# A four-layer image pipeline on one core: six of eight scan convolutions move from TensorE to GpSimd

## The chip, the cores and the metric

One core of a Trainium2 chip runs the program. Its engines work side by side, each through its own queue in order: TensorE (PE, with weight loads shown as PEld), VectorE (DVE), ScalarE (ACT), GpSimd (POOL) and SyncE (SP), which here issues the DMAs. The metric is the device time of one execution in microseconds (us), the median of several.

## The reference

The input is 16 images of 64 channels and 16 x 16 pixels. Four layers follow: an attention over channels; a deformable 3x3 convolution (offsets from a convolution, bilinear samples, batch norm, relu); a softmax attention over the 256 pixels; and a block with layer norm, a depthwise 3x3 convolution, four gated one-dimensional scans, a fuse matmul, a second layer norm and a gated feed-forward. The scans are what this change is about. For each of four directions (left to right, right to left, top to bottom, bottom to top):

```python
y = depthwise 5-tap convolution of seq along the row (or the column) + dw_b
g = sigmoid(seq @ g_w.T + g_b)
o = o + y * g            # then fuse_w, and added to x
```

seq is the depthwise convolution's result, here called y.

## The kernel before

Two images make a pair: their 2 x 64 channels fill the 128 partitions, 256 pixels lie along the row, and there are eight pairs. Each pair runs through some fifty steps. What each engine does, and in which order, is written out by hand in PLAN: a list of tokens step.pair for each engine, walked once. Every step waits on semaphores for its inputs and raises one when it is done. Steps of several pairs are interleaved: while one pair is sampled, the pair before is in its attention and the one before that in its scans. An engine can't pass a waiting step: what stands behind it in the list waits too.

The steps that matter here, with n the pair:

- sp0 to sp8 spread interpolation weights by matmul, ScalarE copies half of them (xe0 to xe8), VectorE multiplies (w0a to w8b, L901, one operand from PSUM, the other from SBUF), and PE samples with the products (s0a to s8b, L534). w8b.n is a pair's last product and s8b.n its last sample. Then relu.n (ScalarE, L747), qk2.n, logit.n, max.n (VectorE, L907, L910), the exponentials, nrm0.n and nrm1.n (the softmax's division, L920), et.n, av.n, x3.n.
- ln1.n: statistics on VectorE, five short 128x1 instructions on GpSimd (L1046 to L1055), the normalization on ScalarE into z_pad. dw.n: two taps of the depthwise convolution on ScalarE; dw2.n to dw8.n: seven on VectorE (L942), each a scalar_tensor_tensor with two SBUF operands. y.n: the two sums added (L951) into y_pad, an image with a border of two.
- gate.n: four matmuls (L602), tanh on ScalarE. scan.n (L615): for each of two axes, five taps, two images, one matmul of 256 columns with a diagonal matrix as weights, two directions side by side in the 128 output partitions; a float32 matmul is two instructions, so 40 in all. ScalarE evicts the scan with its bias into conv (L808). prod.n (VectorE, L957): (tanh + 1) x conv, both in SBUF. fuse.n, x4.n, ln2.n, ff.n, u.n, ff2.n, out.n and the store end the pair.
- dist.n, abs.n, hat.n, hat_y.n (L877, L885) and low.n make the interpolation weights of a later pair. low.n (L1039) is five instructions on GpSimd, whose result feeds PE's transposes tr0.n to tr2.n. x1.n on GpSimd is a copy (L1033).
- hot and warm are matmuls on zeros that fill PE's gaps at both ends.

SP loads x in pairs and stores y_out, each in its order. z_pad, y_pad, dw_acc, gates, conv, prod, z2 and the feed-forward's tiles exist once, so a pair's step waits for the pair before to have used them.

## Time and profile before

| | before |
|---|---|
| median of 3 runs (lowest to highest) | 303.65 us (303.65 to 304.49) |
| span of the profiled execution | 301.8 us |
| PE busy | 287.8 us, 95% |
| VectorE busy | 213.0 us, 71% |
| ScalarE busy | 190.4 us, 63% |
| GpSimd busy | 53.0 us, 18% |
| TensorE clock granted | full in every slice |

The profile is one execution; its own time is the span, and what lies between it and the runs' median is outside the program's instructions. Busy time is the union of an engine's instructions. A timeline row gives the start, the duration, the engine, the line of the kernel, the operation, what it writes and reads, and a count where equal ones are merged; in brackets how long the engine was idle before and who ended it. The chain of waits goes back from the last instruction to what released it, at each step.

### The profile page before, as it was taken

The page shows a single profiled execution, that of the slowest core. Times are in us where ns is not written, and L with a number is a line of the kernel's source. Part 1 is how long each engine was busy: PE and PEld are TensorE (multiplying, and loading weights), DVE is VectorE, ACT ScalarE, POOL GpSimd, SP SyncE. Part 2 cuts the span into 40 slices and gives each one's busy share as a digit, 9 for nine tenths or more (in the row PEclk, how much of TensorE's full clock was granted, in tenths as well). Part 3 has the DMA queues.
Part 4 walks back from the last instruction along what each step waited for, and adds up shares of the span by engine and source line. Part 5 has one row for each costly group of instructions (what it writes and reads, how often), then busy time and mean ns, then how long its engine had stood idle before and what let it go on. Part 6 is the DMA issues. An engine that isn't in the chain of part 4 may idle for free.

```text
span 301.8 us, 7399 instructions
## 1 busy us (share of the span) xinstructions
PE 287.8 (95%) x2870; PEld 183.7 (61%) x2870; DVE 213.0 (71%) x424; ACT 190.4 (63%) x399; POOL 53.0 (18%) x139
## 2 busy tenths in 40 slices
PE   7798999999999999999999999999999999989995
PEld 3555567567555765575767566675565656657742
DVE  3173984779799788858877827687998996655342
ACT  1268757867886569837685654866975755564332
POOL 0332040400140215010222100301421011011110
PEclk9999999999999999999999999999999999999999
DMA  7300000000000000100010001000000000000001
GB/s 235 140 0 20 0 22 2 2 0 2 0 2 3 3 1 2 35 2 0 3 35 2 3 0 31 8 2 1 2 2 0 21 0 3 17 2 0 2 17 35
DMA packets 3057, 4.98 MB, mean 16 GB/s; under 512 B 336, under 2 KB 2768, under 8 KB 2896
## 3 DMA queue, kind: packets, MB, share of 16 engines
q1 hardware_dynamic: 3024, 4.52, 4.7%
q8 instruction: 23, 0.38, 0.6%
q14 instruction: 10, 0.08, 0.1%
HBM read 3.47 MB, written 1.05 MB: 15 GB/s over the span
## 4 chain that ended last, share of the span: by engine, by line
PE 85%; DVE 5%; ACT 5%; issue 3%; POOL 1%; ACTq 0%; POOLq 0%; DVEq 0%
PE ps_cv L534 22%; PE ps_pair L615 11%; PE ps_yb L494 8%; PE ps_pair L480 7%; PE ps_ma L437 6%; PE ps_ma L464 4%; PE ps_mb L580 3%; PE ps_pair L602 3%; PE ps_pair L570 3%; PE ps_mb L591 3%; PE ps_mb L547 3%; PE ps_mb L388 2%; PE ps_pair L635 2%; PE ps_mb L624 2%; PE ps_yb L374 1%
## 5 line engine op out<-in xcount | busy, mean ns | idle before, releaser
L901 DVE TENSOR_TENSOR sb_wt<-ps_yb,sb_xe 128x512 f32<-128x512 f32 x144 | 94.0, 684 | 26.4 <-PE ps_xb L489 24.9
L534 PE MATMUL ps_cv<-sb_wt,sb_w_x 128*64 128x256 f32 x576 | 77.3, 385 | 0.0
L740 ACT ACTIVATE sb_xe<-ps_xb 128x512 f32<-128x512 f32 x72 | 43.0, 597 | 19.3 <-PE ps_xb L489 19.2
L534 PEld LDWEIGHTS ps_cv<-sb_wt,sb_w_x 128*64 128x64 f32 x576 | 38.2, 136 | 20.2 <-issue 7.5
L615 PE MATMUL ps_pair<-sb_y_pad,sb_par 64*128 64x256 f32 x320 | 37.4, 383 | 0.3 <-ACT sb_gates L799 0.3
L615 PEld LDWEIGHTS ps_pair<-sb_y_pad,sb_par 64*128 64x128 f32 x320 | 30.9, 184 | 5.8 <-issue 2.5
L942 DVE SCALAR_TENSOR_TENSOR sb_dw_acc<-sb_z_pad,sb_par,sb_dw_acc 128x256 f32<-128x256 f32 x56 | 25.2, 480 | 9.4 <-ACT sb_dw_acc L792 5.3
L494 PE MATMUL ps_yb<-sb_hats,sb_sel 32*128 32x512 f16 x144 | 29.8, 383 | 0.7
L1039 POOL TENSOR_TENSOR sb_parts<-sb_hat,sb_parts 128x256 f16<-128x256 f32 (+2 forms) x40 | 23.3, 615 | 38.7 <-ACT sb_parts L710 38.6
L1046 POOL TENSOR_SCALAR sb_sc<-sb_mv 128x1 f32<-128x1 f32 x16 | 3.0, 190 | 142.1 <-DVE sb_mv L936 74.7
L489 PE MATMUL ps_xb<-sb_hats,sb_sel 32*128 32x512 f16 x72 | 27.7, 385 | 0.2 <-ACT sb_hats L719 0.2
L730 ACT ACTIVATE sb_w_x<-ps_pair 128x1024 f32<-128x1024 f32 (+1 forms) x24 | 19.4, 810 | 7.7 <-PE ps_pair L480 7.5
L480 PE MATMUL ps_pair<-sb_par,sb_x 64*128 64x256 f32 (+1 forms) x192 | 23.4, 361 | 0.6 <-ACT sb_w_x L730 0.3
L719 ACT ACTIVATE sb_hats<-ps_ma 128x1024 f16<-128x1024 f16 (+1 forms) x24 | 21.1, 880 | 1.7 <-PE ps_ma L464 1.5
L494 PEld LDWEIGHTS ps_yb<-sb_hats,sb_sel 32*128 32x128 f16 x144 | 7.3, 91 | 21.2 <-issue 17.0
L480 PEld LDWEIGHTS ps_pair<-sb_par,sb_x 64*128 64x128 f32 x192 | 15.5, 185 | 7.3 <-issue 6.7
L808 ACT ACTIVATE sb_conv<-ps_pair,sb_par 128x512 f32<-128x512 f32 x16 | 10.1, 683 | 13.1 <-PE ps_pair L615 13.0
L437 PE MATMUL ps_ma<-sb_x_pad,sb_par 128*64 128x128 f32 x288 | 17.4, 274 | 0.3 <-ACT sb_hats L719 0.3
L437 PEld LDWEIGHTS ps_ma<-sb_x_pad,sb_par 128*64 128x64 f32 x288 | 15.8, 136 | 2.3 <-issue 1.6
L769 ACT ACTIVATE sb_b_exp<-ps_pair,sb_b_neg 128x256 f32<-128x256 f32 x32 | 14.8, 473 | 3.0 <-DVE sb_b_neg L910 2.7
L872 DVE TENSOR_TENSOR sb_dist<-ps_ma,sb_grid 128x1152 f32<-128x1152 f32 x8 | 10.8, 1354 | 6.2 <-PE ps_ma L446 6.2
L464 PE MATMUL ps_ma<-sb_sel,sb_parts 128*64 128x128 f16 x320 | 13.8, 222 | 0.0
(117 smaller groups left out, 438.4 us busy)
## 6 DMA issues: line engine op xcount, KB each, us to landing
sb_par<-in_par SPq DMA_DIRECT2D x1, 1519.5 KB, 7.7
sb_x_in<-in_x SPq DMA_DIRECT2D x8, 128.0 KB, 2.1
out_y<-sb_y_out SPq DMA_DIRECT2D x8, 128.0 KB, 1.7
sb_par<-in_par SPq DMA_DIRECT2D x1, 397.0 KB, 4.0
sb_par<-in_par SPq DMA_DIRECT2D x1, 192.0 KB, 3.4
sb_par<-in_par SPq DMA_DIRECT2D x1, 128.0 KB, 2.2
sb_sel<-in_sel SPq DMA_DIRECT2D x1, 128.0 KB, 3.9
```

The lines of the kernel that those rows point to most:

```text
L437: mm = nc.tensor.matmul(ma[C * h:C * (h + 1), 0:P], par_sb[:, a + 2 * OM * t:a + 2 * OM * (t + 1)], x1_pad[:, r:r + HALF_ROWS, t % 3:t % 3 ...
L464: mm = nc.tensor.transpose(bk[columns_of(t), at:at + P], parts[:, 2 * h + b, 4 * g + 2 * t:4 * g + 2 * (t + 1), :, :], ident16)
L480: mm = nc.tensor.matmul(pair[:, 512 * b + PIX * h:512 * b + PIX * h + k], x1[r, P * h:P * (h + 1)], par_sb[r, a:a + k], start=True, stop=True)
L489: return nc.tensor.matmul(xb[:, :], sel_sb[rows, P:2 * P], hats[n % 2][rows, g, :], start=True, stop=True)
L494: return nc.tensor.matmul(yb[h][:, :], sel_sb[rows, P * (2 + h):P * (3 + h)], hats[n % 2][rows, g, :], start=True, stop=True)
L534: mm = nc.tensor.matmul(cv[C * b:C * (b + 1), 0:PIX], w_x[n % 2][:, b, h, k, :], wt_of(n, k, h)[:, PIX * b:PIX * (b + 1)], start=(k == 0 a ...
L615: mm = nc.tensor.matmul(pair[:, 512 * b + PIX * d:512 * b + PIX * (d + 1)], par_sb[r, a:a + P], rows, start=(j == 0), stop=(j == KS - 1))
L719: nc.scalar.activation(hats[n % 2][:, g0:g1, :].rearrange("p g q -> p (g q)"), ma[:, :].bitcast(F16)[:, 0:k], ACT.Copy).then_inc(ev(f"hats ...
L740: nc.scalar.activation(xe[t % XE][:, :], xb[:, :], ACT.Copy).then_inc(ev("xe_ok"), 1)
L901: nc.vector.tensor_tensor(wt_of(n, k, h)[:, :], yb[h][:, :], xe[t % XE][:, :], ALU.mult)\
L942: nc.vector.scalar_tensor_tensor(out=sum_of, in0=dw_source(t), scalar=col("dw_w", t), in1=sum_of, op0=ALU.mult, op1=ALU.add).then_inc(ev(f ...
L1039: nc.gpsimd.tensor_tensor(parts[:, 0:g, a:b, 1, :], hat[:, 0:g, a:b, :], parts[:, 0:g, a:b, 0, :], ALU.subtract).then_inc(ev("low_ok"), 1)
```

## The change

For pairs 1 to 6 the scan is done by GpSimd instead of by PE and ScalarE; pairs 7 and 8 stay as they were. y.n then goes into a plain tile y. GpSimd needs both directions of an axis in the two halves of the partitions, so SP issues four DMAs (dup.n), which copy each image's 64 channels of y to both halves of y_dup. For each axis GpSimd multiplies the middle tap with its weight and adds the bias (mul0), then multiplies each of the four other taps into a scratch tile (mul1 to mul4) and adds it to the sum (sum1 to sum4): 18 instructions a pair over two axes, of 512, 480 or 448 columns, since a tap that reaches past the border is cut. mul13.2 is axis 1, fourth tap, pair 2. prod.n waits for the last sum on both axes. y_pad, z_pad, dw_acc, gates, conv, prod, z2 and the feed-forward's tiles are doubled, x4 has three buffers, x2 eight; the waits look two or three pairs back accordingly, and some waits on older steps are written out. All four orders are new, SP has one of its own, and the zero matmuls at the end are fewer (25 pairs instead of 46). The core of the diff:

```diff
-    ("scan_w", 2 * KS * P), ("scan_b", 2), ("gate_w", 2 * P), ("gate_b", 2), ("fuse_w", C),
+    ("scan_w", 2 * KS * P), ("scan_b", 2), ("scan_c", 2 * KS), ("gate_w", 2 * P), ("gate_b", 2), ("fuse_w", C),
...
+        s1a.8 s1b.8 ff2.4 sp4.8 s2a.8 s2b.8 fuse.5 s3a.8 s3b.8 s4a.8 sp5.8 et1.7 tr2.8 s4b.8 et0.7 sp6.8 ff.5 s5a.8
+        sp7.8 s5b.8 av.7 s6a.8 sp8.8 gate.6 s6b.8 s7a.8 sp_last.8 s7b.8 ff2.5 s8a.8 s8b.8 hot.1 qk2.8 hot.2 logit.8 v2.8
+        hot.3 fuse.6 hot.4 et0.8 gate.7 et1.8 hot.5 av.8 scan.7 hot.6 ff.6 hot.7 gate.8 fuse.7 hot.8 scan.8 ff2.6 hot.9
+        ff.7 fuse.8 hot.10 ff2.7 hot.11 ff.8 hot.12 ff2.8
...
+        w6a.5 out.2 w6b.5 w7a.5 x3.4 st1.4 w7b.5 w8a.5 qk.7 w8b.5 dw2.4 dw4.4 w0a.6 a_max.7 prod.3 a_norm.7 dw6.4 w0b.6
+        x4.3 w1a.6 dw3.4 st2.3 dw5.4 dw8.4 dw7.4 y.4 w1b.6 w2a.6 w2b.6 w3a.6 x1.7 w3b.6 u.3 w4a.6 dist.7 w4b.6 out.3
+        hat.7 hat_y.7 qk.8 w5a.6 w5b.6 w6a.6 a_max.8 a_norm.8 w6b.6 w7a.6 max.5 w7b.6 w8a.6 x1.8 nrm0.5 prod.4 w8b.6
+        w0a.7 nrm1.5 w0b.7 w1a.7 dist.8 w1b.7 w2a.7 x3.5 st1.5 hat.8 w2b.7 w3a.7 hat_y.8 dw2.5 w3b.7 dw3.5 w4a.7 dw5.5
+        dw4.5 w4b.7 dw6.5 dw7.5 max.6 w5a.7 dw8.5 x4.4 y.5 st2.4 w5b.7 w6a.7 nrm1.6 w6b.7 nrm0.6 w7a.7 w7b.7 w8a.7 x3.6
+        st1.6 w8b.7 w0a.8 u.4 w0b.8 w1a.8 dw2.6 dw3.6 dw4.6 w1b.8 dw5.6 dw6.6 w2a.8 dw8.6 dw7.6 w2b.8 y.6 w3a.8 max.7
+        prod.5 out.4 w3b.8 w4a.8 x4.5 nrm1.7 st2.5 w4b.8 nrm0.7 w5a.8 w5b.8 w6a.8 w6b.8 w7a.8 x3.7 st1.7 w7b.8 w8a.8 u.5
+        w8b.8 dw2.7 out.5 dw4.7 dw6.7 dw3.7 dw5.7 prod.6 max.8 dw7.7 dw8.7 x4.6 nrm0.8 y.7 nrm1.8 st2.6 x3.8 st1.8 dw2.8
...
+        grid.1 x1.1 low.1 x1.2 low.2 bn.1 x1.3 x1.4 low.3 ln1.1 low.4 mul10.1 mul00.1 mul11.1 mul01.1 sum01.1 sum11.1
+        x1.5 mul12.1 mul02.1 sum12.1 mul13.1 sum13.1 ln1.2 sum02.1 mul03.1 mul14.1 sum03.1 sum14.1 mul04.1 sum04.1 low.5
+        ln2.1 mul00.2 mul10.2 mul01.2 sum01.2 mul02.2 mul11.2 sum02.2 ln1.3 sum11.2 mul12.2 mul03.2 sum12.2 sum03.2
+        mul13.2 sum13.2 mul04.2 mul14.2 sum04.2 sum14.2 mul10.3 mul00.3 mul11.3 mul01.3 x1.6 sum01.3 sum11.3 mul02.3
+        mul12.3 ln2.2 sum02.3 mul03.3 sum03.3 mul04.3 sum12.3 low.6 sum04.3 ln1.4 mul13.3 sum13.3 mul14.3 sum14.3 ln2.3
+        mul00.4 mul10.4 mul11.4 x1.7 sum11.4 mul01.4 mul12.4 sum12.4 sum01.4 mul02.4 mul13.4 sum02.4 sum13.4 low.7
+        mul14.4 mul03.4 sum03.4 mul04.4 sum04.4 sum14.4 x1.8 ln1.5 low.8 ln2.4 mul10.5 mul11.5 sum11.5 mul00.5 mul01.5
+        mul12.5 sum12.5 ln1.6 sum01.5 mul13.5 mul02.5 sum02.5 mul03.5 sum13.5 sum03.5 mul04.5 mul14.5 sum04.5 sum14.5
+        mul10.6 mul11.6 mul00.6 mul01.6 sum11.6 sum01.6 ln2.5 mul12.6 mul02.6 sum02.6 sum12.6 mul13.6 mul03.6 sum03.6
+        ln1.7 mul04.6 sum13.6 mul14.6 sum04.6 sum14.6 ln2.6 ln1.8 ln2.7 ln2.8
+    """,
+    "sp": """
+        load.3 load.4 load.5 dup.1 load.6 dup.2 dup.3 load.7 load.8 store.1 dup.4 dup.5 dup.6 store.2 store.3 store.4
+        store.5 store.6 store.7 store.8
     """,
...
-HOT = {1: 4, 2: 2, 3: 3, 4: 2, 5: 5, 6: 5, 7: 8, 8: 13, 9: 4}
+BY_POOL = (1, 2, 3, 4, 5, 6)
+ORDER = (2, 1, 3, 0, 4)
+SUMS = 2 * KS - 1
+BY_PE = tuple(n for n in range(1, PAIRS + 1) if n not in BY_POOL)
+HOT = {1: 1, 2: 2, 3: 1, 4: 3, 5: 1, 6: 3, 7: 3, 8: 1, 9: 1, 10: 4, 11: 1, 12: 4}
...
+def done_count(name, n):
+    return sum(k <= n for k in BY_PE) if name == "scan" else n
...
-        z_pad = sb("z_pad", [P, H + 2, PW])
-        dw_acc = [sb(f"dw_acc{i}", [P, PIX]) for i in range(2)]
-        y_pad = sb("y_pad", [P, H + 4, SW])
-        gates = sb("gates", [P, 2, 2, PIX])
-        conv = sb("conv", [P, 2, 2, PIX])
-        prod = sb("prod", [P, 2, 2, PIX])
-
-        x4 = [sb(f"x4{i}", [P, PIX]) for i in range(2)]
+        z_pad = [sb(f"z_pad{i}", [P, H + 2, PW]) for i in range(2)]
+        dw_acc = [[sb(f"dw_acc{i}{t}", [P, PIX]) for t in range(2)] for i in range(2)]
+        y_pad = [sb(f"y_pad{i}", [P, H + 4, SW]) for i in range(2)]
+        y = [sb(f"y{i}", [P, PIX]) for i in range(2)]
+        y_dup = [sb(f"y_dup{i}", [P, 2, H, W]) for i in range(2)]
+        tap_of = [sb(f"tap_of{i}", [P, 2 * PIX]) for i in range(2)]
+        gates = [sb(f"gates{i}", [P, 2, 2, PIX]) for i in range(2)]
+        conv = [sb(f"conv{i}", [P, 2, 2, PIX]) for i in range(2)]
+        prod = [sb(f"prod{i}", [P, 2, 2, PIX]) for i in range(2)]
+
+        x4 = [sb(f"x4{i}", [P, PIX]) for i in range(3)]
         st2, mv2, sc2 = sb("st2", [P, 6]), sb("mv2", [P, 2]), sb("sc2", [P, 5])
-        z2 = sb("z2", [P, PIX])
-        ff_a = sb("ff_a", [P, 2, PIX])
-        ff_g = sb("ff_g", [P, 2, PIX])
-        ff_u = sb("ff_u", [P, 2, PIX])
+        z2 = [sb(f"z2{i}", [P, PIX]) for i in range(2)]
+        ff_a = [sb(f"ff_a{i}", [P, 2, PIX]) for i in range(2)]
+        ff_g = [sb(f"ff_g{i}", [P, 2, PIX]) for i in range(2)]
+        ff_u = [sb(f"ff_u{i}", [P, 2, PIX]) for i in range(2)]
...
+        def made_by(pairs, n):
+            return sum(m <= n for m in pairs)
+
+        def scan_step(n, d, j):
+            return SUMS * made_by(BY_POOL, n) - SUMS + j + 1
...
-            for n in range(3, PAIRS + 1):
-                if n > 5:
-                    store(n - 5)
-                load(n)
-            for n in range(PAIRS - 4, PAIRS + 1):
-                store(n)
+            def dup(n):
+                sp.wait_ge(ev("y_ok"), n)
+                for d in range(2):
+                    wait_past(sp, ev(f"scan_step{d}"), SUMS * made_by(BY_POOL, n - 2))
+                for b in range(2):
+                    for i in range(2):
+                        sp.dma_start(y_dup[n % 2][C * i:C * (i + 1), b, :, :].rearrange("p h w -> p (h w)"),
+                                     y[n % 2][C * b:C * (b + 1), :])\
+                            .then_inc(dup_ok[n % 2], 16)
+
+            walk(PLAN["sp"], {"load": load, "store": store, "dup": dup})
...
-                                              y_pad[r, 2:2 + H, 2:2 + W], start=True, stop=True)
+                                              image(y[n % 2][:, :])[r, :, :] if n in BY_POOL else y_pad[n % 2][r, 2:2 + H, 2:2 + W],
+                                              start=True, stop=True)
...
             def gate(n):
                 act.wait_ge(ev("gate_mm"), n)
-                wait_past(act, ev("prod_ok"), n - 1)
+                wait_past(act, ev("prod_ok"), n - 2)
                 for d in range(2):
-                    last = nc.scalar.activation(gates[:, d, :, :],
+                    last = nc.scalar.activation(gates[n % 2][:, d, :, :],
                                                 pair[:, :].rearrange("p (b d q) -> p b d q", b=2, d=2)[:, :, d, :],
                                                 ACT.Tanh, bias=gate_bh[:, d:d + 1], scale=0.5)
                 last.then_inc(ev("gate_ok"), 1)
 
             def scan(n):
-                act.wait_ge(ev("scan_mm"), n)
-                wait_past(act, ev("prod_ok"), n - 1)
+                act.wait_ge(ev("scan_mm"), made_by(BY_PE, n))
+                wait_past(act, ev("prod_ok"), n - 2)
                 for d in range(2):
-                    last = nc.scalar.activation(conv[:, d, :, :],
+                    last = nc.scalar.activation(conv[n % 2][:, d, :, :],
                                                 pair[:, :].rearrange("p (b d q) -> p b d q", b=2, d=2)[:, :, d, :],
                                                 ACT.Identity, bias=col("scan_b", d))
                 last.then_inc(ev("scan_ok"), 1)
...
             def dw_sum(n):
-                wait_past(dve, ev("gate_mm"), n - 1)
-                wait_past(dve, ev("scan_mm"), n - 1)
+                wait_past(dve, ev("gate_mm"), n - 2)
+                wait_past(dve, ev("scan_mm"), made_by(BY_PE, n - 2))
+                if n - 2 in BY_POOL:
+                    dve.wait_ge(dup_ok[n % 2], 64 * len([m for m in BY_POOL if m <= n - 2 and (n - m) % 2 == 0]))
                 dve.wait_ge(ev("dw_step1"), dw_count(n, TAPS - 2))
                 dve.wait_ge(ev("dw_step0"), dw_count(n, TAPS - 1))
-                nc.vector.tensor_tensor(y_pad[:, 2:2 + H, 2:2 + W], image(dw_acc[0][:, :]), image(dw_acc[1][:, :]),
-                                        ALU.add).then_inc(ev("y_ok"), 1)
+                to = image(y[n % 2][:, :]) if n in BY_POOL else y_pad[n % 2][:, 2:2 + H, 2:2 + W]
+                nc.vector.tensor_tensor(to, image(dw_acc[n % 2][0][:, :]), image(dw_acc[n % 2][1][:, :]), ALU.add).then_inc(ev("y_ok"), 1)
 
             def prod_step(n):
+                wait_past(dve, ev("fuse_mm"), n - 2)
                 dve.wait_ge(ev("gate_ok"), n)
-                dve.wait_ge(ev("scan_ok"), n)
-                nc.vector.scalar_tensor_tensor(out=prod[:, :, :, :].rearrange("p d b q -> p (d b q)"),
-                                               in0=gates[:, :, :, :].rearrange("p d b q -> p (d b q)"), scalar=1.0,
-                                               in1=conv[:, :, :, :].rearrange("p d b q -> p (d b q)"),
+                if n in BY_POOL:
+                    for d in range(2):
+                        dve.wait_ge(ev(f"scan_step{d}"), scan_step(n, d, SUMS - 1))
+                else:
+                    dve.wait_ge(ev("scan_ok"), made_by(BY_PE, n))
+                nc.vector.scalar_tensor_tensor(out=prod[n % 2][:, :, :, :].rearrange("p d b q -> p (d b q)"),
+                                               in0=gates[n % 2][:, :, :, :].rearrange("p d b q -> p (d b q)"), scalar=1.0,
+                                               in1=conv[n % 2][:, :, :, :].rearrange("p d b q -> p (d b q)"),
                                                op0=ALU.add, op1=ALU.mult).then_inc(ev("prod_ok"), 1)
...
-            nc.vector.memset(z_pad[:, :, :], 0.0).then_inc(zero_ok, 1)
-            nc.vector.memset(y_pad[:, :, :], 0.0).then_inc(zero_ok, 1)
+            for i in range(2):
+                nc.vector.memset(z_pad[i][:, :, :], 0.0).then_inc(zero_ok, 1)
+                nc.vector.memset(y_pad[i][:, :, :], 0.0).then_inc(zero_ok, 1)
...
+            def scan_rows(n, d, j):
+                at, to = max(0, j - KS // 2), max(0, KS // 2 - j)
+                m = H - at - to
+                if d == 0:
+                    return (y_dup[n % 2][:, :, :, at:at + m].rearrange("p b h w -> p (b h) w"),
+                            conv[n % 2][:, d, :, :].rearrange("p b (h w) -> p (b h) w", h=H)[:, :, to:to + m],
+                            tap_of[d][:, 0:2 * H * m].rearrange("p (k w) -> p k w", w=m))
+                return (y_dup[n % 2][:, :, at:at + m, :].rearrange("p b h w -> p b (h w)"),
+                        conv[n % 2][:, d, :, W * to:W * (to + m)],
+                        tap_of[d][:, 0:2 * W * m].rearrange("p (b k) -> p b k", b=2))
+
+            def scan_times(d, i):
+                def step(n):
+                    rows, sum_of, tap_to = scan_rows(n, d, ORDER[i])
+                    weight = col("scan_c", KS * d + ORDER[i])
+                    if i == 0:
+                        pool.wait_ge(dup_ok[n % 2], 64 * len([k for k in BY_POOL if k <= n and (n - k) % 2 == 0]))
+                        wait_past(pool, ev("prod_ok"), n - 2)
+                        nc.gpsimd.tensor_scalar(sum_of, rows, weight, col("scan_b", d), ALU.mult, ALU.add)\
+                            .then_inc(ev(f"scan_step{d}"), 1)
+                    else:
+                        pool.wait_ge(ev(f"scan_step{d}"), scan_step(n, d, 2 * i - 2))
+                        nc.gpsimd.tensor_scalar(tap_to, rows, weight, None, ALU.mult).then_inc(ev(f"scan_step{d}"), 1)
+                return step
+
+            def scan_plus(d, i):
+                def step(n):
+                    rows, sum_of, tap_to = scan_rows(n, d, ORDER[i])
+                    pool.wait_ge(ev(f"scan_step{d}"), scan_step(n, d, 2 * i - 1))
+                    nc.gpsimd.tensor_tensor(sum_of, sum_of, tap_to, ALU.add).then_inc(ev(f"scan_step{d}"), 1)
...
+    d["scan_c"] = taps.reshape(2, 2, KS, C).transpose(1, 3, 0, 2).reshape(P, 2 * KS)
```

## Rows read from the trace of the kernel before

**Rows 1.** The page, first table: busy time, share, instructions.
```profile
span 301.8 us, 7399 instructions
PE 287.8 (95%) x2870; PEld 183.7 (61%) x2870; DVE 213.0 (71%) x424; ACT 190.4 (63%) x399; POOL 53.0 (18%) x139
```

**Rows 2.** Timeline of VectorE: w8b.3 and w8b.8 (start, us, engine, line).
```profile
96.83 0.69 DVE L901 TENSOR_TENSOR sb_wt<-ps_yb,sb_xe 128x512 f32<-128x512 f32 x1
...
252.33 0.69 DVE L901 TENSOR_TENSOR sb_wt<-ps_yb,sb_xe 128x512 f32<-128x512 f32 x1 [0.49 <-PE ps_yb L494]
```

**Rows 3.** Busy time of each engine from w8b.3 to w8b.8.
```profile
core 0: us, PE busy (x) PEld busy (x) DVE busy (x) ACT busy (x) POOL busy (x), PEclk, DMA share, GB/s
97.53:253.02 155.49, 154.45 (x1533) 99.11 (x1531) 123.74 (x244) 106.74 (x223) 28.08 (x74) 1.00 0.03 7
```

**Rows 4.** Chain of waits behind the last sample (start, us, what).
```profile
253.84 1.29 PE ps_cv L534 x12
...
255.56 4.61 PE ps_pair L615 x40
260.18 1.01 PE ps_mb L547 x8
...
282.70 4.70 PE ps_pair L615 x40
```

**Rows 5.** Groups by line and shape: xcount | busy us, mean ns | idle before.
```profile
L808 ACT ACTIVATE sb_conv<-ps_pair,sb_par 128x512 f32<-128x512 f32 x16 | 10.1, 683 | 13.1 <-PE ps_pair L615 13.0
...
L957 DVE SCALAR_TENSOR_TENSOR sb_prod<-sb_gates,sb_conv 128x1024 f32<-128x1024 f32 x8 | 9.7, 1218 | 0.3 <-ACT sb_conv L808 0.3
...
L747 ACT ACTIVATE sb_x<-ps_cv,sb_bn_s 128x256 f32<-128x256 f32 x8 | 4.5, 557 | 2.6 <-PE ps_cv L534 2.6
```

**Rows 6.** Groups by line and shape, GpSimd.
```profile
L1039 POOL TENSOR_TENSOR sb_parts<-sb_hat,sb_parts 128x256 f16<-128x256 f32 x28 | 18.2, 680 | 34.1 <-ACT sb_parts L710 34.0
...
L1051 POOL TENSOR_TENSOR sb_sc<-sb_sc,sb_par 128x1 f32<-128x1 f32 x16 | 3.6, 223 | 1.3
L1033 POOL COPY sb_x<-sb_x_pad 128x256 f32<-128x256 f32 x8 | 3.4, 421 | 54.8 <-DVE sb_x_pad L863 40.1 <-PE ps_pair L480 14.7
L1046 POOL TENSOR_SCALAR sb_sc<-sb_mv 128x1 f32<-128x1 f32 x16 | 3.0, 190 | 142.1 <-DVE sb_mv L936 74.7 <-DVE sb_mv L972 67.5
...
L1024 POOL TENSOR_TENSOR sb_grid<-sb_par 128x1152 f32<-128x1152 f32 x1 | 2.1, 2150 | 0.0
```

**Rows 7.** DMA issues (KB each, us to landing).
```profile
sb_x_in<-in_x SPq DMA_DIRECT2D x8, 128.0 KB, 2.1
out_y<-sb_y_out SPq DMA_DIRECT2D x8, 128.0 KB, 1.7
```

**Rows 8.** Timeline of SP: what one issue takes.
```profile
1.15 0.43 SPq L326 DMA_DIRECT2D sb_x_in<-in_x  x1
```

**Rows 9.** Timeline of VectorE and GpSimd at three places.
```profile
112.84 0.76 DVE L877 TENSOR_SCALAR sb_hat<-sb_hat 128x1152 f32<-128x1152 f32 x1 [0.29 <-ACT sb_hat L704]
112.93 0.72 POOL L1051 TENSOR_TENSOR sb_sc<-sb_sc,sb_par 128x1 f32<-128x1 f32 x1
114.31 1.28 DVE L901 TENSOR_TENSOR sb_wt<-ps_yb,sb_xe 128x512 f32<-128x512 f32 x2
...
192.10 2.95 POOL L1039 TENSOR_TENSOR sb_parts<-sb_hat,sb_parts 128x256 f16<-128x256 f32 x5 [9.94 <-ACT sb_parts L710]
193.94 0.76 DVE L856 TENSOR_SCALAR sb_a_nrm<-sb_a_exp,sb_a_rec 128x64 f32<-128x64 f32 x1
...
217.27 3.20 POOL L1039 TENSOR_TENSOR sb_parts<-sb_hat,sb_parts 128x256 f16<-128x256 f32 x5 [0.29 <-ACT sb_parts L710]
217.62 0.34 DVE L910 TENSOR_SCALAR sb_b_neg<-sb_b_max 128x4 f32<-128x4 f32 x1
219.07 0.47 DVE L942 SCALAR_TENSOR_TENSOR sb_dw_acc<-sb_z_pad,sb_par,sb_dw_acc 128x256 f32<-128x256 f32 x1
```

**Rows 10.** Two lines of VectorE: duration ns min/median/max.
```profile
L856 DVE TENSOR_SCALAR sb_a_nrm<-sb_a_exp,sb_a_rec x8: 253/254/762, 8.6 to 193.9; 128x64 f32<-128x64 f32 x8
...
L910 DVE TENSOR_SCALAR sb_b_neg<-sb_b_max x8: 169/169/339, 68.4 to 264.7; 128x4 f32<-128x4 f32 x8
```

194 lines of the change are left out of this document (100 added, 94 removed).

## The prediction

> **What bounds the kernel now.** I read the page's first table: PE is busy for 95% of the span, no other engine above 71% [rows 1]. A mean can hide stages, so I cut the span where the order of the work cuts it, at the end of the last weight product of a pair (w8b) on VectorE: w8b.3 ends at 97.53 us, w8b.8 at 253.02 [rows 2]. In that stretch of 155.49 us (B) PE is busy for 154.45 and VectorE for 123.74, the granted clock is 1.00, that is 2.4 GHz, and GpSimd has 28.08 [rows 3]. So PE alone sets B; five of the eight scans (pairs 1 to 5) lie in it. Ahead of it (A, 97.53 us) there is no scan. Behind it (C, 48.8 us) the chain of waits shows pair 8's latency: its last sample, then 4.61 us of scan.6, which has nothing to do with pair 8 but stands ahead of qk2.8 in PE's order, then qk2, logits, softmax, layer norm, depthwise convolution, scan.8, the rest [rows 4].
>
> The profiled execution's own time is the 301.8 us span; the median of the runs is 303.65, so 1.85 us lies around it, which I leave as it is.
>
> **The change part by part.**
>
> *PE loses six scans.* One takes 4.61 us from its first matmul to the next step's, whether in B or C [rows 4]. In B PE keeps 154.45 - 5 x 4.61 = 131.4, with its 1.04 us of idle time 132.4. ScalarE loses twelve evictions of 0.68 us [rows 5], 8.2 us of an engine that has 106.74 in B [rows 3]; no gain by itself.
>
> *GpSimd gains 18 instructions per pair*: ten multiplications of 448 to 512 columns (mean 474) and eight additions (mean 464). No row has these. For the addition I take the two-input forms: 0.68 us at 256 columns, 2.15 at 1152, 1.64 ns per column, so 1.02 us. For the multiplication the copy: 0.42 at 256, against 0.19 for a multiplication of one column, 0.9 ns per column, so 0.6 [rows 6]. Together 10 x 0.6 + 8 x 1.02 = 14.2 us. Bounds: all 18 at the copy's price, 10.8; all at the addition's, 18.4. I keep 14.2, since each form is priced by its nearest row. The Trainium skill (GPSIMD Engine Reference, Engine selection) calls one-input operations roughly line-rate on GpSimd; at its 1.2 GHz that is an estimate of 0.4 us for the multiplication, under what the copy's rows give, and the scan would be near 12 us.
>
> *The copies of y.* Four DMA issues of 0.43 us each and some 2.1 us to landing, as the loads of x [rows 7, 8]: 3.4 us from y to the first multiplication. SP has long waits, so its time is free; store.2 to store.8 move behind dup.6, but y_out is double, and out.4, the first that needs store.2, stands behind y.6, max.7, prod.5 (1.22 us by itself [rows 5]) and a weight product, against issues and a landing of 1.7 [rows 7, 8]. I cost that at nothing; without that cover it is under 2 us once.
>
> *VectorE's own work.* In the new order B holds 1.8 us more of it (one x4 with its statistics, one u): 125.5. That is under PE's 132.4. But the rows show that the two engines exclude each other. A 128x1 step of GpSimd that takes 0.19 [rows 6] took 0.72 beside VectorE's hat instruction, and ended 0.05 us behind it; five splits took 3.20 instead of 2.95 with one depthwise step among them [rows 9]. The other way round, VectorE's a_nrm (0.25) took 0.76 and b_neg (0.17) took 0.34 while GpSimd split hats [rows 9, 10]. The weight products, which read one operand from PSUM, ran beside GpSimd at their usual length (1.28 for two) [rows 9]. So what counts is VectorE's instructions with two SBUF operands, and its fast tensor_scalar. By the new order there are 86 in B: 35 depthwise steps, 5 y, 5 prod, 5 u, 8 hat, 20 of the softmax's division, 5 b_neg, 3 a_nrm. GpSimd would be at work for (5.5 x 14.2 + 28.08) / 150 = 0.70 of B. One that meets GpSimd waits for half of an instruction (time-weighted 0.87 us) less what its own start hides (b_neg had 0.31 us of GpSimd left and lost 0.17, so 0.14): 0.3 us. Sum 86 x 0.70 x 0.3 = 18 us; I take 17, 0.2 us each. Bounds: 0 (each begins in a gap), and 86 x 0.78 = 67 (each waits for a whole one).
>
> The Trainium skill (SBUF — State Buffer, Who interferes with whom) says that an instruction of VectorE with two SBUF inputs and one of GpSimd that reads SBUF hold a shared port exclusively, and that the second one blocks until the first is done. The rows agree (0.72 us instead of 0.19). Taken to the letter, with nothing hidden, it gives 86 x 0.70 x 0.43 = 26 us; that is the slower rival below.
>
> *A new wait.* prod.n waited for ScalarE's eviction; now it waits for GpSimd's last addition, and everything on VectorE stands behind it, weight products for PE too. Between y.4 and prod.4 VectorE has 14 weight products at 0.60 (two in 1.28, so 0.60 apart [rows 2, 9]) and 7.8 us else: 16.2, with eight lock waits 17.8. GpSimd needs 3.4 + 14.2, and in its order x1.7 and low.7 (0.4 + 3.1) lie in between: 21.1, with its gaps 22.5. So VectorE would wait some 4.7 us. The same count gives 1.7 for pair 1, nothing for 2, 1.3 for 3, 1.0 for 5, 2.6 for 6. One wait gives GpSimd a lead for the next, so of the 8.7 in B I take 6. As a whole GpSimd keeps up: six scans and the older steps between them are 113 us, with 127 gaps of 0.08 (1.3 us over 16 [rows 6]) 123, in some 155.
>
> *Deeper buffers and order* (z_pad, dw_acc, gates, conv, prod, z2, ff tiles, x4): they take out waits for the pair before. Idle PE is 1.04 us in B, so there is no more than that to win. The waits added on the older steps (attn_mm, logit_mm and such, of one or two pairs before) are over long before; nothing. Two more memsets, short ones, lie ahead of VectorE's first input, which comes only with qk.1; nothing.
>
> **The sum.** B: VectorE 125.5 + 17 + 6 + 1.0 idle, as PE has now, = 149.5 instead of 155.5: -6.0. C: qk2.8 no longer stands behind scan.6 but behind ScalarE's relu (0.56 us [rows 5] and its semaphores) and a short filler, so it starts 4.2 us earlier; but prod.6 now stands ahead of max.8 on VectorE and waits 2.6: -1.6. A: 0. 301.8 - 7.6 = 294.2, with 1.85 around it 296.0 us. At 149.5 against PE's 132.4, VectorE is what ends last.
>
> **The rivals.**
>
> 1. *PE stays the bound.* The locks cost little, because GpSimd's access is short or the order keeps the two apart. For it: in the trace of before only two of VectorE's instructions lost time. Against: GpSimd was at 18% then. B is 132.4, C -4.2: 303.65 - 23.1 - 4.2 = 276.4; with some locks, up to 289.
>
> 2. *Slower: the lock puts VectorE past the old time.* Place: the 86 instructions of B; price: 0.3 us each, as with nothing hidden, 26 us, and with it GpSimd's scans are later too, so all 8.7 us of waits at prod: 125.5 + 26 + 8.7 + 1 = 161.2, +5.7, C -1.6 at best: 308. It decides from 0.29 us per instruction on (125.5 + 25 + 6 + 1 = 157.5, two above B, less 1.6 in C). For it: a_nrm lost 0.51 us at once, since GpSimd went straight on from one split to the next; and 35 of the 86 stand directly behind another one. Against: depthwise steps that follow each other hold GpSimd back as well.
>
> 3. *GpSimd can't keep up.* Its queue is strict: low.6 and low.7, which feed PE's transposes, stand among scans 2 to 4. With 18.4 us per scan the whole is 138 + 10, still inside 155, but the waits at prod grow by 4.2 a pair, 20 us less what overlaps; half of it brings B to 159, the time to about 306. It has to be that dear, against the copy's row.
>
> **How the numbers follow.** A measurement of this kernel can tell about 0.3% (0.9 us) from no change. Forecast (289 to 302): 0.42. Rival 1 (276 to 289): 0.20. Rival 2 (302 to 316): 0.30. Rival 3: 0.08. The two slower ones reach back over no change: of their 0.38, 0.05 lies within 0.3%, and 0.33 above; 0.02 of the forecast's own lies within as well. Faster 0.60, same 0.07, slower 0.33. The range leaves out about 0.1 at either end: 281 to 310. The forecast's own is 289 to 302.
>
> **What would show it.** Right: PE's busy time 27 to 28 us lower with idle time in front of samples that wait for weight products; VectorE's depthwise steps at 0.6 to 0.9 us on average instead of 0.47 and its busy time 15 to 20 us higher; prod waiting for GpSimd; GpSimd at about 140 us; qk2.8 about 1 us after the last sample. Wrong: VectorE's steps unchanged and PE still above 95% (rival 1), or depthwise steps at 1 us and VectorE without gaps in a B above 155 us (rival 2); low.6 late and PE waiting for transposes (rival 3). If the granted clock falls below 1.00 with PE's gaps, the rows above don't hold.

## The result: 344.3 us, 13% slower

The changed kernel takes 344.29 us (343.12 to 345.19), the kernel before 304.07 us in the same runs: 1.132 times, 95% interval 1.129 to 1.136. The forecast was 296.

The page's first table of the changed kernel, then three lines of its 40 slices (PE's and GpSimd's busy tenths, and the granted clock in tenths), then the chain of work that ended last, in shares of the span:

```profile
span 343.4 us, 7077 instructions
PE 276.7 (81%) x2588; PEld 166.7 (49%) x2588; DVE 229.9 (67%) x426; ACT 184.8 (54%) x387; POOL 191.9 (56%) x247
...
PE   6879999999996569674878796799984959389874
...
POOL 2020220303179985999998179932479999923011
PEclk9899999999999659998799899699998789879999
...
POOL 38%; PE 37%; issue 10%; DVE 6%; ACT 5%; DMA 2%; SPq 2%; ACTq 0%; POOLq 0%; DVEq 0%
```

Against [rows 1] PE has fallen from 95% to 81%, GpSimd has risen from 53 to 192 us. Over the whole span no engine is near its limit, but GpSimd is at 9 tenths in most slices of the middle and leads the chain. I cut the span as in the prediction, at the last weight product of pairs 3 and 8. Stretch B of the changed kernel, the row that answers to [rows 3] (length; busy us and instructions of PE, weight loads, VectorE, ScalarE, GpSimd; granted clock; DMA):

```profile
98.45:293.09 194.64, 150.62 (x1320) 87.64 (x1320) 138.12 (x248) 102.64 (x213) 156.75 (x174) 0.89 0.05 12
```

B grew from 155.49 to 194.64 us, ahead of it 97.5 became 98.5 and behind it 48.8 became 50.3: the loss is in B. In it VectorE is busy for 138 and idle for 56. GpSimd's 156.75 us of work alone is more than the 149.5 us that I forecast for B. GpSimd's groups (line, operation, shape, count | busy, mean ns | idle before):

```profile
L1141 POOL TENSOR_SCALAR sb_tap_of<-sb_y_dup,sb_par 128x480 f32<-128x480 f32 x24 | 37.3, 1559 | 0.8
L1141 POOL TENSOR_SCALAR sb_tap_of<-sb_y_dup,sb_par 128x448 f32<-128x448 f32 x24 | 34.8, 1454 | 1.0
L1148 POOL TENSOR_TENSOR sb_conv<-sb_conv,sb_tap_of 128x480 f32<-128x480 f32 x24 | 28.7, 1205 | 0.6
L1148 POOL TENSOR_TENSOR sb_conv<-sb_conv,sb_tap_of 128x448 f32<-128x448 f32 x24 | 26.9, 1133 | 0.8
...
L1137 POOL TENSOR_SCALAR sb_conv<-sb_y_dup,sb_par 128x512 f32<-128x512 f32 x12 | 10.7, 895 | 18.2 <-DMA sb_y_dup<-sb_y 18.2
```

The multiplication of one input and one weight (L1141, 1.51 us on average) is dearer than the addition of two inputs (L1148, 1.17), and dearer than the multiplication that also adds the bias (L1137, 0.90 for more columns). A scan is 2 x 0.895 + 8 x 1.507 + 8 x 1.169 = 23.2 us.

What the engines waited for over the whole span (waiter <- releaser: us in total, times, longest):

```profile
ACT sb_z_pad L828 <- POOL sb_sc L1115: 26.8, 7, 6.5
DVE sb_dw_acc L992 <- ACT sb_dw_acc L833: 22.6, 7, 5.5
...
DVE sb_prod L1014 <- POOL sb_conv L1148: 10.9, 4, 3.6
...
PE ps_ma L499 <- POOL sb_parts L1099: 5.7, 3, 4.2
```

and the same waits at z_pad and at the first depthwise step before the change:

```profile
ACT sb_z_pad L785 <- POOL sb_sc L1055: 10.8, 6, 3.1
...
DVE sb_dw_acc L942 <- ACT sb_dw_acc L792: 5.3, 2, 2.7
...
DVE sb_dw_acc L942 <- ACT sb_dw_acc L790: 3.5, 2, 3.0
```

The largest is not prod. It is the layer norm: ln1's five short steps stand in GpSimd's list behind multiplications and additions of another pair's scan, ScalarE waits for them ahead of z_pad, and VectorE waits for ScalarE at the first depthwise step. One case, pair 2. VectorE's timeline ends the statistics at 102.79 us:

```profile
102.61 0.18 DVE L986 BATCH_NORM_AGGREGATE sb_mv<-sb_st 128x2 f32<-128x6 f32 x1
...
113.91 0.76 DVE L992 SCALAR_TENSOR_TENSOR sb_dw_acc<-sb_z_pad,sb_par,sb_dw_acc 128x256 f32<-128x256 f32 x1 [5.52 <-ACT sb_dw_acc L833]
...
121.47 1.61 DVE L1014 SCALAR_TENSOR_TENSOR sb_prod<-sb_gates,sb_conv 128x1024 f32<-128x1024 f32 x1 [3.01 <-POOL sb_conv L1148]
```

GpSimd's timeline meanwhile is at pair 1's scan, without a gap, and comes to ln1.2 at 110.96:

```profile
103.38 3.23 POOL L1141 TENSOR_SCALAR sb_tap_of<-sb_y_dup,sb_par 128x480 f32<-128x480 f32 x2
106.58 1.20 POOL L1148 TENSOR_TENSOR sb_conv<-sb_conv,sb_tap_of 128x480 f32<-128x480 f32 x1
107.87 1.79 POOL L1141 TENSOR_SCALAR sb_tap_of<-sb_y_dup,sb_par 128x448 f32<-128x448 f32 x1
109.75 1.12 POOL L1148 TENSOR_TENSOR sb_conv<-sb_conv,sb_tap_of 128x448 f32<-128x448 f32 x1
110.96 0.19 POOL L1106 TENSOR_SCALAR sb_sc<-sb_mv 128x1 f32<-128x1 f32 x1
```

So 1.3 us of work comes 8.2 us late, and VectorE is idle for 5.5 us there and for 3.0 more at prod.1. The same just behind B: pair 8's relu (L785) stands on ScalarE behind ln1.7's z_pad, which waits for GpSimd. VectorE waits for the same z_pad at the first depthwise step of pair 7, and out.5 (L1043) stands behind that step; out.5 reads a tile in PSUM that qk2.8 is to write:

```profile
296.55 0.60 ACT L828 ACTIVATE sb_z_pad<-sb_x,sb_sc 128x256 f32<-128x256 f32 x1 [4.21 <-POOL sb_sc L1115]
...
298.09 0.55 ACT L785 ACTIVATE sb_x<-ps_cv,sb_bn_s 128x256 f32<-128x256 f32 x1
...
297.82 1.45 DVE L992 SCALAR_TENSOR_TENSOR sb_dw_acc<-sb_z_pad,sb_par,sb_dw_acc 128x256 f32<-128x256 f32 x1 [4.73 <-ACT sb_dw_acc L833]
299.20 0.47 DVE L1043 SCALAR_TENSOR_TENSOR sb_y_out<-ps_mb,sb_par,sb_x 128x256 f32<-128x256 f32 x1
```

PE is idle for 5.4 us ahead of qk2.8, which begins 5.6 us after the last sample, where I had about 1. What ends the wait is out.5, a microsecond behind the relu:

```profile
299.82 1.97 PE L582 MATMUL ps_mb<-sb_x,sb_par 128*64 128x256 f32 x8 [5.36 <-DVE sb_y_out L1043]
```

### The profile page after: what moved, and what is told of

Same layout as the page of the kernel before. It is cut to its first block, busy times and chain, and to the rows that moved or that the text cites. A ratio compares the mean times of both kernels' runs of the same rounds, so it can differ in the third digit from the quotient of the medians.

```text
span 343.4 us, 7077 instructions
## 1 busy us (share of the span) xinstructions
PE 276.7 (81%) x2588; PEld 166.7 (49%) x2588; DVE 229.9 (67%) x426; ACT 184.8 (54%) x387; POOL 191.9 (56%) x247
## 4 chain that ended last, share of the span: by engine, by line
POOL 38%; PE 37%; issue 10%; DVE 6%; ACT 5%; DMA 2%; SPq 2%; ACTq 0%; POOLq 0%; DVEq 0%
POOL sb_tap_of L1141 17%; POOL sb_conv L1148 12%; PE ps_cv L569 8%; PE ps_pair L515 3%; PE ps_ma L472 3%; POOL sb_conv L1137 3%; PE ps_yb L529 3%; PE ps_pair L651 3%; PE ps_ma L499 2%; PE ps_pair L605 2%; DMA sb_y_dup<-sb_y 2%; SPq L377 2%; POOL sb_sc L1109 2%; PE ps_mb L582 1%; PE ps_yb L409 1%
## 5 line engine op out<-in xcount | busy, mean ns | idle before, releaser
L569 PE MATMUL ps_cv<-sb_wt,sb_w_x 128*64 128x256 f32 x576 | 85.3, 403 | 4.8 <-issue 3.3
L1141 POOL TENSOR_SCALAR sb_tap_of<-sb_y_dup,sb_par 128x480 f32<-128x480 f32 (+1 forms) x48 | 72.0, 1507 | 1.8
L1148 POOL TENSOR_TENSOR sb_conv<-sb_conv,sb_tap_of 128x480 f32<-128x480 f32 (+1 forms) x48 | 55.6, 1169 | 1.3
L992 DVE SCALAR_TENSOR_TENSOR sb_dw_acc<-sb_z_pad,sb_par,sb_dw_acc 128x256 f32<-128x256 f32 x56 | 32.5, 617 | 22.8 <-ACT sb_dw_acc L833 22.6
L515 PE MATMUL ps_pair<-sb_par,sb_x 64*128 64x256 f32 (+1 forms) x192 | 25.8, 390 | 10.8 <-ACT sb_w_x L769 7.4
L515 PEld LDWEIGHTS ps_pair<-sb_par,sb_x 64*128 64x128 f32 x192 | 16.9, 202 | 19.1 <-issue 14.3
L1137 POOL TENSOR_SCALAR sb_conv<-sb_y_dup,sb_par 128x512 f32<-128x512 f32 x12 | 10.7, 895 | 18.2 <-DMA sb_y_dup<-sb_y 18.2
L660 PE MATMUL ps_mb<-sb_prod,sb_fuse_h 128*64 128x256 f32 x64 | 10.4, 453 | 11.9 <-DVE sb_prod L1014 7.5
L472 PE MATMUL ps_ma<-sb_x_pad,sb_par 128*64 128x128 f32 x288 | 18.8, 285 | 0.7 <-DVE sb_x_pad L910 0.7
L828 ACT ACTIVATE sb_z_pad<-sb_x,sb_sc 128x256 f32<-128x256 f32 x8 | 4.8, 604 | 26.8 <-POOL sb_sc L1115 26.8
```

Source lines behind the costliest of these rows:

```text
L472: mm = nc.tensor.matmul(ma[C * h:C * (h + 1), 0:P], par_sb[:, a + 2 * OM * t:a + 2 * OM * (t + 1)], x1_pad[:, r:r + HALF_ROWS, t % 3:t % 3 ...
L515: mm = nc.tensor.matmul(pair[:, 512 * b + PIX * h:512 * b + PIX * h + k], x1[r, P * h:P * (h + 1)], par_sb[r, a:a + k], start=True, stop=True)
L569: mm = nc.tensor.matmul(cv[C * b:C * (b + 1), 0:PIX], w_x[n % 2][:, b, h, k, :], wt_of(n, k, h)[:, PIX * b:PIX * (b + 1)], start=(k == 0 a ...
L992: nc.vector.scalar_tensor_tensor(out=sum_of, in0=dw_source(n, t), scalar=col("dw_w", t), in1=sum_of, op0=ALU.mult, op1=ALU.add).then_inc(e ...
L1141: nc.gpsimd.tensor_scalar(tap_to, rows, weight, None, ALU.mult).then_inc(ev(f"scan_step{d}"), 1)
L1148: nc.gpsimd.tensor_tensor(sum_of, sum_of, tap_to, ALU.add).then_inc(ev(f"scan_step{d}"), 1)
```

## The experiments

All are built on the changed kernel (e4 on the one before). A lone `...` in a diff, or at the end of a line, marks code left out. "B" is the stretch defined above, cut in each trace at the same two weight products.

**e1_two_op: the same product, written with two operations.**

```diff
-nc.gpsimd.tensor_scalar(tap_to, rows, weight, None, ALU.mult) ...
+nc.gpsimd.tensor_scalar(tap_to, rows, weight, 0.0, ALU.mult, ALU.add) ...
```

> The 48 tap multiplications of GpSimd, written with a second operation (add 0.0), nothing else changed. In the changed kernel the multiplication with one operation took 1.51 us on average for 448 to 480 columns, the one with multiply and add 0.76 undisturbed for 512. Theory 1, the form: GpSimd has a slow path for a tensor_scalar with a single operation; the 48 fall from 1.51 to about 0.75, GpSimd's busy time from 192 to about 155 us, and the time by 25 to 36 us, to 308 to 320. Rival, the shape: cut rows and strides make them slow, and they stay at 1.4 to 1.5 us and the time at 344.

315.50 us, 1.0405 (1.036 to 1.045): 28.8 us less for adding a zero. The groups of GpSimd in e1:

```profile
L1141 POOL TENSOR_SCALAR sb_tap_of<-sb_y_dup,sb_par 128x480 f32<-128x480 f32 x24 | 16.9, 710 | 0.8
L1141 POOL TENSOR_SCALAR sb_tap_of<-sb_y_dup,sb_par 128x448 f32<-128x448 f32 x24 | 16.6, 696 | 1.0
```

0.70 us instead of 1.51; a scan is 2 x 0.85 + 8 x 0.70 + 8 x 1.20 = 16.9 us. And B of e1:

```profile
98.22:269.26 171.04, 145.86 (x1320) 84.55 (x1320) 143.70 (x247) 102.32 (x214) 124.14 (x179) 0.93 0.05 14
```

The form of the instruction, changed by itself, is worth 28.8 us, the largest of the causes that these runs tell apart. But e1 is still slower than the kernel before: with the multiplication near the price that I assumed, and the scan inside my bounds (10.8 to 18.4), the forecast would still have been 19.5 us too low.

**e4_prices: six instructions side by side**, on 480 columns, set into GpSimd's list of the kernel before at three places.

```diff
+nc.gpsimd.tensor_scalar(to[0][:, :], src, by, None, ALU.mult)
+nc.gpsimd.tensor_scalar(to[1][:, :], src, by, 0.0, ALU.mult, ALU.add)
+nc.gpsimd.tensor_scalar(to[2][:, :], src, 0.5, None, ALU.mult)
+nc.gpsimd.tensor_scalar(to[3][:, :], src, 0.5, 0.0, ALU.mult, ALU.add)
+nc.gpsimd.tensor_copy(to[4][:, :], src)
+nc.gpsimd.tensor_tensor(to[5][:, :], src, par_sb[:, a + 480:a + 960], ALU.add)
```

> The kernel before with six extra GpSimd instructions at three places, on tiles of their own, 480 contiguous columns each: multiply by a column of scalars, one operation; the same with add 0.0 behind it; the first two with immediates instead of a column; a copy; an addition of two tiles. Theory 1, the form: the single operation with a column costs about 1.48 us although nothing is strided, its two-operation form about 0.72. Rival, the shape: both about 0.7. The copy 0.58, the addition 1.1 to 1.2. The time is about that of before, since GpSimd sits idle there.

GpSimd's timeline at the first place, L1066 to L1071 in that order:

```profile
60.24 1.49 POOL L1066 TENSOR_SCALAR sb_dum<-sb_par 128x480 f32<-128x480 f32 x1
61.71 0.67 POOL L1067 TENSOR_SCALAR sb_dum<-sb_par 128x480 f32<-128x480 f32 x1
62.45 1.41 POOL L1068 TENSOR_SCALAR sb_dum<-sb_par 128x480 f32<-128x480 f32 x1
63.83 0.59 POOL L1069 TENSOR_SCALAR sb_dum<-sb_par 128x480 f32<-128x480 f32 x1
64.37 0.59 POOL L1070 COPY sb_dum<-sb_par 128x480 f32<-128x480 f32 x1
64.93 1.21 POOL L1071 TENSOR_TENSOR sb_dum<-sb_par 128x480 f32<-128x480 f32 x1
```

With one operation a tensor_scalar takes 1.4 to 1.5 us, whether the factor is a column or a constant; with two it takes 0.6 to 0.7, near the copy. (Its single time was 310.0 us, beside 303.4 for the kernel before, where I had expected about the same; I didn't follow that up.)

**e2_one_tap: GpSimd computes only the middle tap** (four of five taps missing from the output); order, buffers and copies of y unchanged.

```diff
-SUMS = 2 * KS - 1        # and mul01..04, mul11..14, sum01..04, sum11..14 in the list
+SUMS = 1
```

> The changed kernel without the four outer taps: GpSimd does only the first multiplication on each axis, 2 instructions a pair instead of 18, so the scan leaves out 4 of 5 taps. Order, buffers and DMAs are as they were. Theory 1, the length of GpSimd's scans is the whole loss: with 127 us of work off its queue, PE is the bound again, and the time is 276 to 288 (303.65 - 23.1 - 4.2 = 276.4 as the lower end). VectorE's depthwise steps fall from 0.617 to about 0.48. Rival, the new order, the deeper buffers or the copies cost by themselves: the time stays above 300.

288.45 us, 0.951 (0.948 to 0.955), half a microsecond above what I expected. B of e2:

```profile
97.44:241.87 144.43, 135.28 (x1320) 79.52 (x1320) 125.54 (x248) 102.22 (x214) 39.48 (x88) 1.00 0.06 16
```

So neither the order nor the copies nor the buffers are the loss; it is GpSimd's work on the outer taps. VectorE's 125.54 is its own work with little of GpSimd beside it, as I had counted (125.5). In e1 it has 143.70: 18.2 us more, where I had 17 for the shared access. The other 8.4 us of e1's longer B are idle time: 27.3 us of VectorE's, against 18.9 in e2.

**e5, e6, e9, e13: which part of GpSimd's time.** e1 stays 27 us above e2. Three suspects: prod waits for the last addition; GpSimd's access to memory holds VectorE up; the layer norms and splits stand behind the scans in GpSimd's list.

e5_unread is e1 with the additions put into a tile that nobody reads, so that prod waits for the first tap only (four taps missing from the output):

```diff
-dve.wait_ge(ev(f"scan_step{d}"), scan_step(n, d, SUMS - 1))
+dve.wait_ge(ev(f"scan_step{d}"), scan_step(n, d, 0))
...
-nc.gpsimd.tensor_tensor(sum_of, sum_of, tap_to, ALU.add) ...
+nc.gpsimd.tensor_tensor(aside_of(n, d, ORDER[i]), aside_of(n, d, ORDER[i]), tap_to, ALU.add) ...
```

> As e1 (two-operation multiplications), but the additions go into a tile that nobody reads, and prod waits only for the first tap of each axis: four of the five taps are missing from the output. GpSimd does the same work on the same amount of data, VectorE no longer waits for its end. e1 took 315.5 us and e2 (one tap, same order) 288.5: 27 us are to be split. Theory, the shared access: VectorE's busy time stays near e1's 235 us and the time near 308 to 316, since prod's wait was a small part in e1 (PE waited 5.2 us for prod). Rival, the wait of prod for the last addition: 300 us or less with VectorE still near 235.

315.28 us, as e1. But this run could free little: with e1's shorter scans VectorE stands idle at prod for only 0.2 us in all (10.9 in the changed kernel).

e6_tiny keeps e1's list and waits and puts instructions on one column, about as long, in place of those on whole rows (four taps missing):

```diff
-nc.gpsimd.tensor_scalar(tap_to, rows, weight, None, ALU.mult) ...
+nc.gpsimd.tensor_tensor(spin[:, 4 * d:4 * d + 1], bn_s[:, 0:1], half[:, :], ALU.pow)
+nc.gpsimd.tensor_tensor(spin[:, 4 * d + 1:4 * d + 2], bn_s[:, 0:1], bn_s[:, 0:1], ALU.mult) ...
...
-nc.gpsimd.tensor_tensor(sum_of, sum_of, tap_to, ALU.add) ...
+nc.gpsimd.tensor_tensor(spin[:, 4 * d + 2:4 * d + 3], bn_s[:, 0:1], half[:, :], ALU.pow)
+nc.gpsimd.tensor_tensor(spin[:, 4 * d + 3:4 * d + 4], bn_s[:, 0:1], half[:, :], ALU.pow) ...
```

> As e1, but each of the 48 multiplications and 48 additions of whole rows on GpSimd is put in place by two instructions on 128x1 elements of about the same length together (a power of 0.55 us and a product of 0.19 for 0.70; two powers, 1.1, for 1.2): four of the five taps are missing from the output. GpSimd's queue is as long as e1's, prod, the layer norms and the splits of hats wait as there, but GpSimd hardly touches the memory. Theory, the shared access: VectorE's busy time falls from e1's 235 us to e2's 215 and the time to 289 to 297. Rival, the queue (what stands behind the scans on GpSimd, and prod): VectorE at 215 too, but the time at 306 to 314.

308.46 us, 1.015 (1.012 to 1.018): 7 us below e1, in the range of the rival, the queue. The depthwise steps of e1, then of e6 (count | busy us, mean ns | idle before):

```profile
L992 DVE SCALAR_TENSOR_TENSOR sb_dw_acc<-sb_z_pad,sb_par,sb_dw_acc 128x256 f32<-128x256 f32 x56 | 36.5, 688 | 11.8 <-ACT sb_dw_acc L833 11.6
...
L993 DVE SCALAR_TENSOR_TENSOR sb_dw_acc<-sb_z_pad,sb_par,sb_dw_acc 128x256 f32<-128x256 f32 x56 | 25.5, 493 | 12.6 <-ACT sb_dw_acc L834 12.4
```

B of e6, with GpSimd as busy as in e1 and VectorE back near e2's, and what VectorE waits for at prod:

```profile
99.07:261.81 162.74, 139.76 (x1320) 82.41 (x1320) 127.35 (x247) 102.27 (x214) 123.04 (x270) 0.97 0.06 14
...
DVE sb_prod L1015 <- POOL sb_spin L1152: 7.0, 5, 2.6
```

e9_unread_order is e5 with GpSimd's list rewritten: x1, ln1, low and ln2 stand where they become ready in e2, the scans fill the rest.

```diff
-        x1.5 mul12.1 mul02.1 sum12.1 mul13.1 sum13.1 ln1.2 sum02.1 mul03.1 mul14.1 sum03.1 sum14.1 mul04.1 sum04.1 low.5
...
+        sum01.1 mul12.1 mul02.1 ln1.2 sum12.1 sum02.1 mul13.1 mul03.1 sum13.1 sum03.1 mul14.1 low.5 ln2.1 mul04.1
...
```

> As e5 (two-operation multiplications, additions into an unread tile, prod waits only for the first tap, four of five taps missing from the output), and GpSimd's list is rewritten: each layer norm, split of hats and copy of x1 stands where it would be ready if the scans took no time, the scan's instructions fill what is left. e5 took as long as e1 (315), e6 with the same queue and almost no memory access 308.5, e2 without the queue 288.5. Theory, GpSimd's strict queue: the 20 us between e6 and e2 are the layer norms and splits that stand behind the scans; freed here together with prod, the time falls to e2 plus the shared access's 7 to 8 us, 293 to 300. Rival, the cause is not in the order of GpSimd's list: 308 to 316 as before.

307.2 us, the middle of its three shortest runs, of which the traced one is one, 1.008 (1.004 to 1.013); the other five took 309.7 to 312.4. That is less of a gain than I expected. B of e9:

```profile
97.65:259.05 161.40, 141.38 (x1321) 82.86 (x1320) 145.11 (x248) 102.79 (x214) 125.25 (x175) 0.96 0.06 14
```

e13_tiny_free takes both away: e9's list with e6's instructions.

> As e9 (GpSimd's list with the layer norms, splits and x1 ahead, prod not waiting for the last addition, four of five taps missing from the output), with e6's short 128x1 instructions in place of the multiplications and additions: GpSimd's queue is as long in time as in e1, nothing waits for its end, and it hardly touches the memory. From the last weight product of pair 3 to that of pair 8 e5 took 170.3 us, e6 (no memory) 162.7, e9 (list) 161.4, e2 144.4. Theory, memory and queue are the whole loss: this stretch at 144 to 148, the time at 288 to 292, and the 9 us that the two single savings don't explain appear when both are taken. Rival, the savings only add: 153 in the stretch, 297 to 300, and something third is left.

289.45 us, 0.954 (0.953 to 0.956), within 1 us of e2 although GpSimd is busy for 121.7 us in B:

```profile
97.36:243.71 146.35, 135.19 (x1321) 79.51 (x1320) 125.34 (x248) 102.24 (x214) 121.71 (x263) 1.00 0.06 16
```

The four lengths of B make a table:

| | list as in the change | urgent steps ahead, prod free |
|---|---|---|
| GpSimd reads and writes rows | 171.0 (e1; e5 170.3) | 161.4 (e9) |
| GpSimd on one column | 162.7 (e6) | 146.3 (e13) |

Memory access and list (with prod freed) together are all but 1.9 us of the loss against e2 (144.4). Alone they give back 8.3 and 9.6 us, both give 24.7: the savings more than add. Two things that change along with them may have a part in that, and no run separates them: once the memory access is gone, VectorE waits for GpSimd at prod (7.0 us in e6), and the granted clock goes from 0.93 in e1 over 0.97 and 0.96 to 1.00. The waits show the list's part: VectorE's idle time at the first depthwise step is 8.8 us before the change, 22.6 us in the changed kernel, 11.6 in e1, 11.6 in e5, 12.4 in e6, and 6.0 in e2, e9 and e13. The row of e13, over the whole span:

```profile
DVE sb_dw_acc L993 <- ACT sb_dw_acc L834: 6.0, 5, 3.0
```

**e15_three: scans of three taps** (two of five taps missing from the output). Its list leaves out the instructions of the other two.

```diff
-SUMS = 2 * KS - 1
+SUMS = 5
```

> As e1 with three of the five taps (two of them missing from the output): a scan is 2 x 0.77 + 4 x 0.70 + 4 x 1.2 = 9.1 us of GpSimd instead of 17. Theory, each microsecond of GpSimd costs its share (e2 with 1.5 us 288.5, e1 with 17 315.5, so 1.74 us of time for each us of a scan): 302. Rival, a threshold: with 9 us the scans fit between y and prod beside the splits and layer norms, so no waits, and only the shared access is left: 289 to 294.

300.62 us, 0.992 (0.989 to 0.995): no sign of a threshold at 9 us, as the rival had it. By the durations in each trace, between scans of 1.6 us (e2, 288.5), 9.4 (300.6), 16.9 (e1, 315.5) and 23.2 (the change, 344.3) the time rises by 1.6, 2.0 and 4.6 us for each us of a scan. An estimate on that line: a scan would have to stay under some 10.8 us (9.4 + 2.85 / 2.0) for the kernel only to equal the one before.

**Misses.** Four runs (e8, e10, e11, e12) asked whether other lists would save the idea; two, e3 and e7, whether the new order is sound with the scans on PE.

e3_none_pool puts all scans back on PE in the new order, right behind the gates; e7_none_b puts them where the shared bank of PSUM is free. Besides the lists, from which the copies of y are gone in both, the edit is:

```diff
-BY_POOL = (1, 2, 3, 4, 5, 6)
+BY_POOL = ()
```

> The changed kernel with all eight scans on PE again (behind their gates, scan.1 five steps later), no copies of y; the new order of everything else and the deeper buffers stay. Theory 1: the order itself costs little; PE has its 23 us back and sets the time, 300 to 308. Rival, the order is bad even without GpSimd: over 312.

> The new order, buffers and copies, but all eight scans on PE as before the change, each scan put at a place where the bank of PSUM that it shares with the gates has been read (in e3 it stood directly behind the gates and cost 22.7 us). Theory, order and buffers neither gain nor lose much: 297 to 306 us with PE at 287 and the clock at 1.00. Rival, the new order is worth something only without the scans on PE, or is bad by itself: over 310.

326.12 us (1.072 to 1.082) and 319.44 (1.047 to 1.056). Better places gave 6.7 us, but both are above the kernel before: B is 176.1 us in e7 with PE idle for 12 of it, against 1.04 in [rows 3]. Whether the new order is worse or my places for the scans are, these two don't tell.

e8_123 leaves the scans of pairs 1 to 3 on GpSimd, those of 4 to 6 on PE:

> The new order with the scans of pairs 1 to 3 on GpSimd (two-operation multiplications) and those of pairs 4 to 8 on PE. Theory, shared access: half of the scans cost half of what they cost in e1, about 10 us on VectorE, and PE loses 3 x 4.6 us: between 300 and 309, about the time before (303.4). Rival, only the length of GpSimd's queue counts: with half of the scans there is slack, so e7 less up to 13.8 us, 293 or less.

318.58 us (1.046 to 1.051), above both expectations; it carries e7's trouble with it and decides nothing.

e10_order rewrites GpSimd's list for the whole computation as far as prod allows; e11_chain and e12_chain also move prod and what follows it later in all lists, by up to 8 and up to 4 us:

```diff
-        w0b.4 x3.2 w1a.4 st1.2 w1b.4 w2a.4 hat.5 w2b.4 w3a.4 hat_y.5 dw2.2 w3b.4 w4a.4 dw4.2 dw3.2 dw6.2 w4b.4 prod.1
...
+        w5a.4 dw5.2 dw8.2 dw7.2 y.2 nrm1.3 w5b.4 prod.1 w6a.4 nrm0.3 w6b.4 x4.1 st2.1 w7a.4 w7b.4 w8a.4 x3.3 st1.3
```

(VectorE's lists of e10 and e11 at prod.1.)

> As e1, whole computation, with GpSimd's list rewritten as far as the other lists allow: a layer norm or split that VectorE only releases behind prod stays behind that pair's scan. A count with GpSimd's measured durations (17 us a scan, from y to prod some 20 in the other lists with 2 to 5 us of splits and layer norms between) makes each scan 2 to 4 us late, 19 us over six pairs, with this list as with the old one. Theory: no gain, 311 to 317. Rival, the old list is what was bad: 300 to 306.

> As e10, and everything that follows a pair's scan (prod, fuse, x4, second layer norm, feed-forward, out) stands 5 to 8 us later in the lists of all engines for pairs 1 to 5, behind work of other pairs, with the layer norms and splits ahead of the scan's instructions as in e9; whole computation. Theory, GpSimd has time enough (124 us of 171) and only the lists make others wait for it: 293 to 302, faster than the 303.4 before. Rival, the shared access and the gaps follow wherever it is put: 308 or more.

> As e11 with the shift limited to 4 us. Theory: between e10 and e11, 298 to 306, since each scan would still be late by up to 4 us. Rival: as e10.

318.4 us (1.041 to 1.052), 342.53 (1.126 to 1.132) and 332.49 (1.092 to 1.099). e10 gained nothing, as the count said, and its trace adds something to e9: the layer norms come early again (VectorE's idle time at the first depthwise step is 6.0 us, as in e2), but VectorE waits 7.1 us at prod instead of 0.2, PE waits 9.9 for prod instead of 2.9, and the depthwise steps take 0.73 us instead of 0.69. B is 170.3 us, near e1's 171.0: where prod needs the last addition, a better list moved the wait and did not remove it. e11 and e12 went the wrong way: the later the chain, the slower. In e11 PE is idle for 14.3 us (2.6 in e10) ahead of the softmax's transposes (L615), 11.0 of it until VectorE's x4 and y_out have read a tile in PSUM that they share. That is a part; I didn't find out how much each of the moved steps costs. No experiment with the whole computation beats the kernel before.

## Why the prediction was wrong

**The step that failed first** is the price of the multiplication: "For the multiplication the copy ... so 0.6". It measured 1.51 us. The bound failed with it: "all at the addition's, 18.4" took the two-input form for the dearest, and a scan took 23.2; the addition itself was 1.17 instead of 1.02. GpSimd had "about 140 us" to do, and did 192. No row of before shows a one-operation tensor_scalar on GpSimd: the one on 128x1 [rows 6] multiplies by 1.0 as a second operation. e1 and e4 show that it is the form alone: 28.8 of the 48.3 us by which the forecast missed.

**The second** is in "A new wait" and in the sum. I looked for who waits for the scan (prod) and not for who stands behind it in GpSimd's list: ln1, which feeds z_pad and with it VectorE's depthwise steps, and the splits. The wait at prod that I did count is there in the changed kernel, 10.9 us with a scan 9 us dearer (I had 8.7 in B and took 6); in e1 it is 0.2, and the layer norms are still late. In e1, with the multiplication at 0.70, B is 171.0 instead of my 149.5: VectorE's busy time is 143.7 (I had 142.5), its idle time 27.3 where I had 7.0. These 20 us are the other 19.5, but for small changes ahead of B and behind it. They have two parts: 8.4 come with the outer taps, and 11.9 VectorE has in e2 too (18.9 of idle time): the sum let it run without any gap but prod's and PE's old 1.0.

**The size of the lock was near, in part by luck.** I had 17 us of lost time on VectorE; e1 has 18.2, the changed kernel 12.6 (138.1 - 125.5). My working has the loss grow with GpSimd's share of the time and with the length of its instructions; in the changed kernel both are larger than in e1 (0.81 of B against 0.73; 1.51 us a multiplication against 0.70) and the loss is smaller, so that working isn't borne out, and no run says why. Depthwise steps, 0.47 us in [rows 9], take 0.62 on average there and 0.69 in e1, within the 0.6 to 0.9 I had named. And I added the loss to VectorE's own time as if it stood alone; the table shows that lock and list together cost more than the sum of the two.

**PE's floor.** I had 132.4 for B if PE stayed the bound; e2 and e13, with nearly nothing from GpSimd in the way, have 144.4 and 146.3, PE being busy for 135.3 and 135.2 (I had 131.4). The new order leaves PE 9 to 11 us of gaps, where I had kept the 1.04 of before.

**The clock.** I named it as what would void the rows: the granted clock in B is 0.89 in the changed kernel, 0.93 in e1, 1.00 in e2 and e13. The same 1320 matmuls take 150.6, 145.9, 135.3 and 135.2 us. (1.00 is 2.4 GHz.) In the slices above it falls to 5 and 6 tenths in and just behind slices in which PE's busy share falls, and e13, with 11 us of gaps instead of 44, has it at full. The deepest fall is the case of pair 2 above. PE's last matmul before it ends at 109.3 us; PE is idle for 5.75, waiting for ScalarE, which waits for ln1.2, and then runs at 0.50, that is 1.2 GHz, for the next 12 us:

```profile
115.05 2.08 PE L515 MATMUL ps_pair<-sb_par,sb_x 64*128 64x256 f32 x8 [5.75 <-ACT sb_w_x L769]
...
114.00:126.00 12.00, 7.56 (x33) 4.34 (x35) 8.66 (x12) 5.33 (x13) 11.16 (x11) 0.50 0.00 0
```

So a late layer norm is paid for twice here, by the wait and by slower matmuls behind it. How much of the 15.3 us of longer matmuls lay on the path no run separates.

**The rivals.** Rival 3 named the mechanism, "GpSimd can't keep up. Its queue is strict", at 0.08 and 306 us, with a scan of 18.4 us; the scan was 23.2, and the waits behind the layer norms are larger than those behind low. PE did wait for transposes, 5.7 us, the sign that I had named. I gave it little because it had to be "that dear, against the copy's row": one wrong price decided both the forecast and the chance. Rival 2 needs VectorE without gaps, and it has 56 us of them.

**What held, and a small miss:** VectorE's own work, and the stretch ahead of B (98.5 against 97.5). The copies of y were dearer than 3.4 us: y.1 ends at 91.27, the first multiplication begins at 96.08, 4.8 us later, since the four issues alone take 3.28 (SP's timeline) where I had 4 x 0.43 from a single one:

```profile
91.30 3.28 SPq L377 DMA_DIRECT2D sb_y_dup<-sb_y  x4
```

## What to carry to other kernels

Before work is given to an idle engine, read that engine's list and ask who stands behind the new instructions: short steps on which others wait turn its idle time into latency that the chain needs, and here each us of a scan cost 1.6 to 4.6 us over six pairs. Price every instruction in its exact form, or measure it first: a form that no row shows can't be bounded by a neighbour that looks dearer. And when an engine at 95% loses work, don't expect the whole of it back: here the new lists left PE 9 to 11 us of gaps in B even where GpSimd was out of the way, and with 25 (e1) and 44 us of them the granted clock was 0.93 and 0.89.

## What the runs showed of the hardware

A tensor_scalar on GpSimd with one operation takes 1.49 us on 480 float32 columns and 1.41 with a constant; the same with a second operation that adds zero takes 0.67 and 0.60, a copy 0.59, an addition of two inputs 1.20 (e4, means of three). The prediction's sentence on the Trainium skill (GPSIMD Engine Reference, Engine selection: one-input operations roughly line-rate) fits the two-operation form and the copy better, and not the one-operation form. The other one (SBUF — State Buffer, Who interferes with whom) agrees with the traces: with GpSimd at work on rows VectorE's depthwise steps take 0.69 us (e1), with it as busy on single columns 0.49 (e6).
